# Attention scores from 64 rows for each head, as row tiles, with half of the second normalisation on VectorE and the router's result in a score bank

## The reference

```python
q = xpos_apply(split_heads((layernorm(x) @ Wq.T + bq) * D ** -0.5), downscale=False)
k = xpos_apply(split_heads(ctx @ Wk.T + bk), downscale=True)
v = split_heads(ctx @ Wv.T + bv)
attn = softmax(q @ k.T) @ v
x = x + tanh(g_xattn) * (attn @ Wo.T + bo)

def mole(x, W, b, A, Bm, Rw):              # E = 3 experts, rank R = 8
    gates = softmax(x @ Rw)
    z = einsum('bsd,edr->ebsr', x, A) * gates
    return x @ W + b + einsum('ebsr,erh->bsh', z, Bm) / 8

n = layernorm(x)
x = x + tanh(g_ffn) * mole(relu(mole(n, W1, b1, A1, B1, R1)), W2, b2, A2, B2, R2)
```

## Time and profile before

| | |
|---|---|
| median of 3 runs | 575.08 us (574.99 to 575.38) |
| the profiled execution, its own time | 568.85 us |
| its span, first to last instruction | 567.0 us |
| TensorE busy | 502.2 us (89%) |
| VectorE busy | 392.3 us (69%) |
| ScalarE busy | 216.5 us (38%) |
| chain that ended last | TensorE 50%, VectorE 28%, ScalarE 10%, DMA 5%, issue 4% |

### The profile page before, as it was taken

How to read it: one execution, slowest core, us unless ns; L and a number is a source line. 1 busy time by engine, 2 the same in 40 slices (tenths; PEclk the granted TensorE clock), 3 DMA queues, 4 the chain that set the end, 5 groups by cost and what they waited for, 6 DMA issues and landing times.

```text
span 567.0 us, 7820 instructions
## 1 busy us (share of the span) xinstructions
PE 502.2 (89%) x3032; PEld 372.0 (66%) x3032; DVE 392.3 (69%) x904; ACT 216.5 (38%) x357; POOL 64.4 (11%) x113
## 2 busy tenths in 40 slices
PE   2478865999989898999989898999989998989897
PEld 1345344855967387845967487855977487847787
DVE  4757475858879387958878487958888486934633
ACT  3233512463335613463325513453326513361330
POOL 2336002010110102010101002010201001010100
PEclk9955976999999999999999999999999999999999
DMA  8391044011702062112702061113602071110001
GB/s 296 51 223 39 1 89 61 2 50 56 94 0 76 7 118 27 40 49 62 88 0 77 25 105 21 39 50 69 82 1 76 1 97 15 43 36 2 1 37 38
DMA packets 13329, 31.86 MB, mean 56 GB/s; under 512 B 1732, under 2 KB 2572, under 8 KB 13164
## 3 DMA queue, kind: packets, MB, share of 16 engines
q1 hardware_dynamic: 6983, 14.63, 15.2%
q10 hardware_dynamic: 6309, 16.73, 11.0%
HBM read 14.31 MB, written 4.19 MB: 33 GB/s over the span
## 4 chain that ended last, share of the span: by engine, by line
PE 50%; DVE 28%; ACT 10%; DMA 5%; issue 4%; POOL 2%; SPq 0%; ACTq 0%; DVEq 0%; POOLq 0%
PE psF L1099 13%; PE psX L1128 6%; PE psX L1199 5%; ACT probs L547 4%; DMA qT<-probs 4%; DVE max_t L750 4%; DVE probs L675 4%; PE psO L1213 3%; PE psF L1145 3%; ACT xn L431 3%; PE psO L1216 3%; DVE ln_s L601 2%; PE psX L1028 2%; PE psF L1105 2%; DVE probs L682 2%
## 5 line engine op out<-in xcount | busy, mean ns | idle before, releaser
L750 DVE TENSOR_REDUCE max_t<-psX 128x4 fp32r<-128x616 f32 x128 | 99.2, 795 | 9.1 <-PE psX L1128 7.4
L547 ACT ACTIVATE probs<-psX 128x1024 f32<-128x1024 f32 x64 | 64.3, 1025 | 50.8 <-PE psX L1199 50.8
L1145 PE MATMUL psF<-w_hi,h_hi 128*128 128x284 f32 (+1 forms) x240 | 72.1, 300 | 0.0
L1128 PE MATMUL psX<-km,qT 96*128 96x308 f32 x256 | 64.9, 343 | 8.1 <-DMA qT<-probs 4.2
L1145 PE MATMUL psF<-w_lo,h_hi 128*128 128x284 f32 (+1 forms) x240 | 70.4, 293 | 0.0
L1145 PE MATMUL psF<-w_hi,h_lo 128*128 128x284 f32 (+1 forms) x240 | 70.2, 292 | 0.0
L1128 PEld LDWEIGHTS psX<-km,qT 96*128 96x128 f32 x256 | 48.1, 206 | 24.1 <-DVE max_t L750 9.7
L463 ACT ACTIVATE h_hi<-psF 128x512 fp32r<-128x512 f32 x59 | 34.3, 593 | 54.4 <-PE psF L1105 54.4
L1145 PEld LDWEIGHTS psF<-w_hi,h_hi 128*128 128x128 f32 x240 | 45.2, 188 | 4.9 <-issue 4.8
L1145 PEld LDWEIGHTS psF<-w_hi,h_lo 128*128 128x128 f32 x240 | 45.2, 188 | 0.1
L1099 PE MATMUL psF<-xT_lo,w_hi 128*128 128x512 f32 x118 | 45.2, 398 | 0.0
(11 more groups left out here) (181 smaller groups left out, 931.6 us busy)
## 6 DMA issues: line engine op xcount, KB each, us to landing
qT<-probs SPq DMA_DIRECT2D x32, 256.0 KB, 9.9
qT<-probs ACTq DMA_DIRECT2D x16, 256.0 KB, 7.6
x<-in_x_dram ACTq DMA_DIRECT2D x8, 512.0 KB, 3.2
x_ln<-in_x_dram ACTq DMA_DIRECT2D x7, 512.0 KB, 3.4
out_dram<-x ACTq DMA_DIRECT2D x7, 512.0 KB, 3.1
turn<-in_turns_dram SPq DMA_DIRECT2D x2, 512.0 KB, 10.1
heads_t<-in_w_dram SPq DMA_DIRECT2D x1, 1024.0 KB, 8.2
heads_t<-in_w_dram SPq DMA_DIRECT2D x1, 994.0 KB, 14.1
```

The costliest lines, as they stand in the source:

```text
L547: nc.scalar.activation(dst, psX[:, 2 * (i % 2):2 * (i % 2) + 2, :], ACT.Exp).then_inc(sc_exp.sem, 1)
L750: V.tensor_reduce(max_t[:, k, half, :].rearrange("p (h g) -> p g h", h=2)[:, 2 * j:2 * j + 2, :], psX[:, 2 * j:2 * j + 2, 0:2 * S].rearran ...
L1128: ins = mm(psX[:, g % 4, 0:2 * S], qT[0:KS, g, tokens(k)], km[0:KS, g, :, :].rearrange("p h s -> p (h s)"), start=True, stop=True)
L1145: ins = mm(out_bank(d, k)[:, cs], a[:, m, tokens(k)], w[:, m, cs], start=m == 0 and i == 0, stop=m == HT - 1 and i == 2)
```

## The change

- **64 rows for each head.** `qT` grows to 128 partitions. The first head of a pair has rows 0 to 47 (16 high, 16 low, 16 high) and its maximum in row 48, the second the same from row 64 on. The queries are now moved by twelve DMAs of 128 KB, each from 64 partitions to 8 (`q_dst`), eight on SP's queue and four on ScalarE's, and one small DMA clears row 48 before the rough scores.
- **Score pairs as row tiles.** A main score matmul contracts over 49 rows that lie within one half of the array, and those of the two heads of a pair stand one behind the other and write different banks. The rest scores take sixteen such matmuls instead of eight. The rough scores contract over 112 rows instead of 96.
- **The values in smaller pieces.** `values` is cut in `values_rest` and four parts, each over two head pairs, and `project_q` stands behind all of them. On VectorE `head_blocks(d, 2)` and `q_products` move to the start of the next step.
- **The second normalisation** of tiles 2 and 3 is done by VectorE (`normalise2`).
- **The router in a score bank.** `router1` writes psX bank 3 instead of psF bank 1, so that `hidden_main(d, 0)` need not wait until its result has been read; `max_scores(c, 1)` waits for that instead.

```diff
-KS = 96
-KA = KS + 2
+HR = 64
+KM = 3 * D
+KX = HR + KM
...
-        qT = sb("qT", [KA, NG, CH], F32R)
+        qT = sb("qT", [P, NG, CH], F32R)
...
-        km = sb("km", [KA, NG, 2, S], F32R)
-        kr = sb("kr", [KA, NG, P], F32R)
+        km = sb("km", [P, NG, 2, S], F32R)
+        kr = sb("kr", [P, 2, 5 * P], F32R)
...
+        def q_dst(hh, t, s):
+
+            r = HR * hh + D * t + D // 2 * s
+            return qT[r:r + D // 2, :, :].bitcast(F32)
...
-                    sp.dma_start(qT[16 * s:16 * s + 16, :, :].bitcast(F32),
-                                 probs[:, 4 + s, :]).then_inc(q_rows.sem, 16)
+                    for hh in range(2):
+                        sp.dma_start(q_dst(hh, 0, s), probs[64 * hh:64 * hh + 64, 4 + s, :]).then_inc(q_rows.sem, 16)
+                sp.dma_start(qT[KM:KM + 1, :, :].bitcast(F32), zero[:, :].bitcast(F32)).then_inc(q_rows.sem, 16)
                 for s in range(2):
                     sp.wait_ge(q_lo.sem, q_lo.at(c, s + 1))
-                    sp.dma_start(qT[32 + 16 * s:48 + 16 * s, :, :].bitcast(F32),
-                                 probs[:, s, :]).then_inc(q_rows.sem, 16)
+                    for hh in range(2):
+                        sp.dma_start(q_dst(hh, 1, s), probs[64 * hh:64 * hh + 64, s, :]).then_inc(q_rows.sem, 16)
 
...
                     act.wait_ge(q_hi.sem, q_hi.at(c, s + 1))
-                    act.dma_start(qT[64 + 16 * s:80 + 16 * s, :, :].bitcast(F32),
-                                  probs[:, 4 + s, :]).then_inc(q_rows.sem, 16)
+                    for hh in range(2):
+                        act.dma_start(q_dst(hh, 2, s), probs[64 * hh:64 * hh + 64, 4 + s, :]).then_inc(q_rows.sem, 16)
 
...
+            def normalise2(d, u):
+
+                dve.wait_ge(ln2_rstd.sem, ln2_rstd.at(d, 1))
+                if d is not LAST:
+                    dve.wait_ge(xT_ps.sem, xT_ps.at(d + 1))
+                for k in (2, 3):
+                    V.tensor_scalar(xn[:, k, :], x1[:, u, k, :], ln_m[:, 1, k, 0:1], ln_r[:, 1, k:k + 1],
+                                    ALU.subtract, ALU.mult).then_inc(ln2_out_v.sem, 1)
...
+                else:
+                    head_blocks(d, 2)
                     head_blocks(d, 3)
                     head_norm(d, 1)
                     head_back(d, 1)
+                    q_products(c, u)
+                    head_low(d, 1)
                     q_turn(c)
-                    head_low(d, 1)
                     q_low(c)
-                else:
-                    head_blocks(d, 3)
-                    head_norm(d, 1)
-                    q_low(c)
-                    head_back(d, 1)
-                    head_low(d, 1)
                 if first:
                     key_operands(b)
...
+            def transpose_x2(d, bank=2):
+
+                for n, k in enumerate((0, 2, 1, 3)):
+                    done = ln2_out_v if k >= 2 else ln2_out_a
+                    pe.wait_ge(done.sem, done.at(d, k % 2 + 1))
                     for f in range(FT):
-                        ins = nc.tensor.transpose(psX[:, 2 + f, tokens(k)], xn[:, k, P * f:P * f + P], ident)
-                        if k == TT - 1:
...
             def router1(d, second=False):
 
-                if not second and d is not LAST:
-                    pe.wait_ge(y_out.sem, y_out.at(d - 1, 2))
...
+                            z = psX[32 * k:32 * k + 32, 3, 0:P]
                             ins = mm(z, a1_sb[:, f, :], a[:, f, tokens(k)].bitcast(F32), start=n == 0, stop=n == 3)
                         n += 1
...
                     if m >= 3:
                         pe.wait_ge(w1_lo_s.sem, w1_lo_s.at(d, m - 2))
-                    elif m == 0:
-                        pe.wait_ge(g1_v.sem, g1_v.at(d, 1))
                     elif not second:
                         pe.wait_ge(y_out.sem, y_out.at(d - 1, m + 2))
...
                 if i == 0:
                     pe.wait_ge(q_rows.sem, q_rows.at(c))
+                if i == 1 and c:
+                    pe.wait_ge(g1_v.sem, g1_v.at(c - 1, 1))
                 if i >= 2:
                     pe.wait_ge(max_red.sem, max_red.at(c, i - 1))
...
-                    if kind == "rest":
-                        g = 2 * (n + j)
-                        mm(o_ps, kr[:, g, :], qT[:, g, :], start=True, stop=False)
-                        ins = mm(o_ps, kr[:, g + 1, :], qT[:, g + 1, :], start=False, stop=True)
-                    else:
-                        ins = mm(o_ps, km[:, n // 2, j, 0:P], qT[:, n // 2, :], start=True, stop=True)
+                if kind == "rest":
+                    for k in range(4):
+                        for hh in range(2):
+                            rows = slice(HR * hh, HR * hh + KM + 1)
+                            ins = mm(psX[:, 2 * (i % 2) + hh, :], kr[rows, n // 2, P * k:P * k + P], qT[rows, 2 * n + k, :],
+                                     start=k == 0, stop=k == 3)
+                else:
+                    for hh in range(2):
+                        rows = slice(HR * hh, HR * hh + KM + 1)
+                        ins = mm(psX[:, 2 * (i % 2) + hh, :], km[rows, n // 2, hh, 0:P], qT[rows, n // 2, :],
+                                 start=True, stop=True)
                 ins.then_inc(sc_ps.sem, 1)
 
-            def values(c, g, first, last):
...
+            def values_rest(c, g, first, last):
+
+                pe.wait_ge(sc_exp.sem, sc_exp.at(c, (1, 1, 6, 6)[g]))
...
+                        pe.wait_ge(const_v.sem, 7)
...
+                    pe.wait_ge(xT_lo_s.sem, xT_lo_s.at(c + 1, 1))
...
-                    h = 4 * g + j
-                    ins = mm(pv_bank(g)[32 * j:32 * j + 32, :], v_sb[:, h, :], probs[:, h % 8, :], start=False, stop=True)
...
+                for p in (2 * part, 2 * part + 1):
+                    for hh in range(2):
+                        g, j = 2 * (p // 4) + hh, (p + 2 * hh) % 4
+                        ins = mm(pv_bank(g)[32 * j:32 * j + 32, :], v_sb[:, 4 * g + j, :], probs[:, 2 * (p % 4) + hh, :],
+                                 start=False, stop=True)
                 ins.then_inc(pv_ps.sem, 1)
 
             def step(b, u, first=False, second=False, last=False):
@@ -1225,12 +1258,15 @@
                     pe.wait_ge(wkv_loaded.sem, 16)
...
                     pe.wait_ge(x1_s.sem, x1_s.at(d))
                     max_scores(c, 0)
                     router1(d, second)
-                    max_scores(c, 1)
+                    hidden_main(d, 0, second, (0,))
                     if full:
                         lora2_operand(e, 1)
-                    hidden_main(d, 0, second, (0,))
+                    max_scores(c, 1)
...
+                scores(c, 0)
+                max_transposed(c, 1, first)
+                scores(c, 1)
+                if last:
+                    pe.wait_ge(w1_hi_s.sem, w1_hi_s.at(d))
+                    pe.wait_ge(w1_lo_s.sem, w1_lo_s.at(d))
+                    out_tile(LAST - 1, 2, 0, 3)
+                else:
+                    if not first:
+                        pe.wait_ge(w1_lo_s.sem, w1_lo_s.at(d))
+                    transpose_x(c + 1, psF[:, 1:3, :], ln1_out, xT_ps)
+                scores(c, 2)
+                values_rest(c, 0, first, last)
+                scores(c, 3)
+                values_rest(c, 1, first, last)
+                scores(c, 4)
+                values(c, 0)
+                if u == 1 and not last:
+                    ctx_transposed(b + 1, ctx_sb)
+                scores(c, 5)
+                scores(c, 6)
+                values(c, 1)
+                scores(c, 7)
+                if u == 1 and not last:
+                    project_k(b + 1)
+                if last:
+                    out_tile(LAST - 1, 2, 3, 5)
+                scores(c, 8)
+                values_rest(c, 3, first, last)
+                scores(c, 9)
+                values_rest(c, 2, first, last)
+                values(c, 2)
+                if last:
+                    out_tile(LAST - 1, 2, 5, 8)
+                values(c, 3)
                 if not last:
-                    pe.wait_ge(sc_exp.sem, sc_exp.at(c, 9))
                     project_q(c + 1, False)
-                values(c, 3, first, last)
-
```

222 lines of the change are left out of this document (103 added, 119 removed).

## The result

The changed kernel takes 682.8 us (680.9 to 686.0), the kernel before 575.0 us in the same comparison: a ratio of 1.194, 95% interval 1.188 to 1.201. The profiled execution's own time is 685.95 us and its span 683.8, 116.8 more than before. My sum, made against the profiled execution, gave +83.7: the direction and the cause were forecast, and 33 us are missing in the size. A part of these 33 us is the choice of executions: the profiled one was the fastest of the kernel before (568.85 us, median 575) and the slowest of the changed kernel. By the medians the change costs 107.8 us, and the forecast of 658.8 us is 24 us short. In the comparisons of the experiments the same kernel before has medians of 570.7 to 572.1 us, and each ratio is against the runs beside it.

What follows compares the result with a forecast made beforehand. TensorE, busy 89%, bounds the kernel, with query rows only 2.9 us behind as slack; slower transfer makes M0 wait. Step terms sum to +83.7 on 568.85, 652.6; plus 6.2 to the median, 658.8, said as 658; range 606 to 702 us.

Steps and rivals of the forecast that it cites:

- One of the signs: Score stage, profile after: main score pairs 0.25 us apart; at 0.47 us the forecast would be off by 30.
- The larger memory clearing at the start costs nothing.: Start of the kernel: the larger clearing costs or brings nothing of its own while M0 waits for the rows.
- I take 25 us, near the halving.: Query-row transfer: 25 us instead of 11.7, as DMAs to 8 partitions run at about half the rate.
- 13.3 - 3.4: Step 1, which already waits for rows: 13.3 us more, less 3.4 from the score stage, +9.9.
- sixteen main matmuls cost eight, -1.9 us: Score stage: the two main matmuls of a pair take the time of one, saving 1.9 us.
- The last score stage, -3.4.: Last score stage, with no query rows behind it: shorter by the whole stage gain, 3.4 us.
- The queues collide: Rival on the query-row transfer: both queues gain nothing from each other, 28.9 us of transfer, 690 us; chance 0.18.
- The row tiles do not run together: Rival on the score stage: pairs do not overlap, 3.8 us more eight times, 689 us; chance 0.10.
- The rows as fast as before: Rival on the query-row transfer: a DMA's rate depends on bytes alone, so the kernel gets faster, 545 us; chance 0.09.
- Decides below about 15 us of transfer: Query-row transfer: under about 15 us the kernel gets faster; above, later M0 and low clock eat the gain.
- ScalarE's issues are hidden: ScalarE's four DMA issues instead of two: statistics about 2 us late, covered by the wait for the rows.
- without that cover 1 us a step: ScalarE's extra DMA issues: 1 us a step if the wait for the rows did not cover them.

Runs made afterwards that it cites:

- b_split8: The kernel before with only its six query-row moves cut in two, from 128 to 16 partitions into twice 64 to 8: 642.6 us, 1.125 times the kernel before.
- a_rows16: The changed kernel with six query-row DMAs from 128 to 16 partitions in place of the twelve: 570.9 us, ratio 1.001 to the kernel before.
- a_full_rows: a_spread8 with its main score matmuls contracting over all 128 rows instead of the 64 of one head: 555.2 us, ratio 0.974 to the kernel before.
- a_spread8: The changed kernel with six query-row DMAs, each writing 16 rows eight apart over both halves: 556.4 us, ratio 0.974 to the kernel before.
- a_no_act: The changed kernel without ScalarE's four query-row DMAs, leaving eight on SP's queue: 608.6 us, ratio 1.068 to the kernel before.
- a_act_other_half: The changed kernel with ScalarE's four moves issued second head first, on the other half of the partitions: 661.1 us, ratio 1.158 to the kernel before.
- a_stride3: The changed kernel with each head's 48 rows interleaved, so each of twelve DMAs writes 8 rows three apart: 581.0 us, ratio 1.017 to the kernel before.

## Why the prediction was right, and where it was short

The forecast's mechanism holds in its main points. M0 waits for query rows in every step (forecast some 14 us; measured 10.9 to 16.6 behind step 0). The first issue hardly moves (22.6; 23.4). The clock falls in the hole and M0 to M2 takes 8.0 us (8.4). The stage is shorter by 2.3 us (3.4). One of the signs did not come: the main score pairs start 0.33 to 0.43 us before what stands behind them, and not 0.25. b_split8 and a_rows16 show that the DMAs' shape is the cause.

The missing 33 us by my own terms:

| term | forecast | measured |
|---|---|---|
| step 0 | +13.3 | +23.0 |
| step 1 | +9.9 | +15.5 |
| steps 2, 4, 6 | +29.4 | +35.4 |
| steps 3, 5, 7 | +34.5 | +41.5 |
| last score stage | -3.4 | +1.4 |
| sum | +83.7 | +116.8 |

- *"The larger memory clearing at the start costs nothing."* Wrong: the first issue of step 0 is at 29.1 instead of 22.7 us, +6.4. I had excused it by M0's wait, but it stands ahead of the transfer, not beside it.
- *"I take 25 us, near the halving."* Right: 25.7 us from the first to the last packet in steps 1 to 7 (28.4 in step 0). Short was what stands around it: the sum let M0 begin with the last packet, 26.2 us behind the issue, and it came at 27.8, and at 30.6 in step 0. That is 1.6 us in seven steps and more in the first.
- *Step 1: "13.3 - 3.4".* I moved the first issue forward with the stage. It came 2.2 us later than before (28.6 against 26.5 from the stage's start), since the heads' work now stands ahead of the queries. I had seen this for the other steps and not for this one.
- *The stage: "sixteen main matmuls cost eight, -1.9 us".* They run together and it brings nothing (a_full_rows). Of the 2.3 us that the stage gained, 1.3 are the holes for exponentials (1.6 us before, 0.4 now); the other 1.0 came with the new order of the products and was not priced by itself. So 18.4 and not 17.3, and the first issue 0.8 to 1.1 us later than forecast. With keys the holes were only 0.9 us before, which my 1.6 for every stage overlooked; and the 17.3 there for the end of `values` has no working in the prediction (by its own terms 22.4 - 3.4 - 2.75 is 16.3), it was 18.0.
- *"The last score stage, -3.4."* Measured +1.4, and 0.0 in a_spread8. There the output projection begins 1.6 us earlier behind the stage's start than before, the first layer 1.0 us earlier, and by the first layer's end nothing of it is left. A part goes where TensorE's clock is at 0.50 in that trace (519.0 to 522.4): the router still starts 1.8 us earlier, the first layer behind it 1.0. Where the rest goes I did not take apart. The 1.4 us of the changed kernel appear behind the first layer, where its trace has TensorE's clock at 0.50 for 3.4 us and that of before has not.

**The bounds and the rivals.** "The queues collide" was put at 28.9 us of transfer with 0.18. Its size did not come (25.7 us by the packets, within the forecast's 22 to 27), but its mechanism did: a_no_act shows that ScalarE's queue adds its full 9.0 us, and a_act_other_half that 2.6 of this are the same place in memory. The rest of it fits two queues that share eight engines. So that 25 us was hit is in part luck: I had halved each rate and let the queues still gain from each other; they gain nothing, and SP's queue alone is faster than half, 65 GB/s by the packets of a_no_act against 54.5. "The row tiles do not run together" is false, though of the gain that it denied nothing came. "The rows as fast as before" was priced at 545; made real in a_spread8 it is 556.4. Of my terms for it the steps without keys held (-3.5 measured for -4.2), the steps with keys did not (-1.0 for -3.6: their stage is only 1.5 us shorter, and TensorE waits 0.5 us for gates), nor did the last stage, and step 0 is 5.0 us later. "Decides below about 15 us of transfer" was wrong: at 13.4 us (a_rows16) there is no change, and at 12.3 (a_stride3) it was still slower by 1.7%.

**The issues.** "ScalarE's issues are hidden" was right only under the cover of M0's wait, and "without that cover 1 us a step" was too little: 3.8 us in each step with keys.

**The rule of the Trainium skill** (DMA: Bandwidth & Descriptors, "Why a DMA increments its semaphore by 16 and not by 1") gives eight engines for these DMAs, and the closing packets agree. But I let the rate follow from it, and a_stride3 moves the same data on eight engines in half the time. The page that puts the runs in the right order is the one I gave to a rival: the Trainium skill (SBUF — State Buffer, "Door 1: The DMA port swizzle") puts four neighbouring partitions on one port, so that 8 rows side by side reach two and 16 reach four. The traces agree in this order: 18 to 36 GB/s at one row, 55 to 65 at eight side by side, 109 at sixteen side by side, up to 188 and 374 for spread rows on two queues.

## What to carry to other kernels

When a DMA inside SBUF writes few partitions, look at where they lie before counting engines: from the first issue to the last packet of step 5 the same data took 26.5, 13.9, 13.4 or 8.7 us by the choice of destination rows and of how many DMAs they were cut into, and a free order of contraction rows makes that choice free. When a stage becomes shorter, follow the data that the next stage waits for, not the engine that became free; here the query rows took back all of it in every second step until they were spread. And look at what a change adds at the start: in a_rows16 step 0 lost 7.2 us, about as much as all other steps gained together. Price a small matmul in its surroundings: pairs that run together between products of another shape saved nothing.
